# Scattering the weighted FFN rows with addition onto the result in DRAM, instead of reading them back and combining them

## What is computed

```python
gout = x @ Wgate + bgate
topv, topi = jax.lax.top_k(gout, K)              # K = 2 of E = 8 experts
topw = jax.nn.softmax(topv, axis=-1)
combine = jnp.sum(jax.nn.one_hot(topi, E) * topw[..., None], axis=-2)
z = (x @ W1[e] + b1[e]) * (x @ W2[e] + b2[e])    # for each expert e
g = z @ Wg[e] + bg[e]
o = g * sigmoid(g) * (z @ Wl[e] + bl[e])
y = o @ W3[e] + b3[e]
out = einsum('bse,bseh->bsh', combine, y)        # weighted sum of a row's two experts
x = x + attention(xn) + out
```

## Time and profile before

| | |
|---|---|
| median of three runs | 509.82 us |
| the profiled execution's own time | 512.48 us |
| its span in the trace | 510.1 us |
| busy: PE, DVE, ACT, POOL | 401.6, 286.8, 157.0, 228.0 us |
| first gather of the layer-1 FFN starts | 315.4 us |
| its last scatter starts | 487.59 us |
| last entry in the chain that ended last | 503.29 us |

### The profile page before, as it was taken

One profiled execution on the slowest core, in us unless ns is written; L12 is line 12 of the kernel. 1 busy time (PEld: TensorE's weight loads), 2 busy tenths in 40 slices (PEclk: granted clock), 3 DMA queues, 4 the chain that ended last, 5 costly groups with the idle time before them and its releaser, 6 DMA issues.

```text
span 510.1 us, 8068 instructions
## 1 busy us (share of the span) xinstructions
PE 401.6 (79%) x2156; PEld 290.2 (57%) x2157; DVE 286.8 (56%) x791; ACT 157.0 (31%) x414; POOL 228.0 (45%) x341
## 2 busy tenths in 40 slices
PE   2877788999989999476429958799999999998800
PEld 0666677978887877365417626545555555554400
DVE  5246967767657762000084798556666665555514
ACT  1522333434433334133106231232323222222212
POOL 8336516165256234536313012225565666666222
PEclk9988899999999999879759997999999999999955
DMA  8750000000000001967242000001111100001053
GB/s 290 248 229 0 2 1 2 1 0 1 2 2 0 1 21 61 383 243 259 68 152 84 1 0 12 21 12 33 36 31 34 33 31 31 31 31 36 21 155 107
DMA packets 23130, 34.49 MB, mean 68 GB/s; under 512 B 2784, under 2 KB 18400, under 8 KB 22848
## 3 DMA queue, kind: packets, MB, share of 16 engines
q1 hardware_dynamic: 19264, 25.89, 14.7%
q0 software_dynamic: 3840, 8.26, 5.2%
HBM read 26.35 MB, written 7.80 MB: 67 GB/s over the span
## 4 chain that ended last, share of the span: by engine, by line
PE 26%; POOL 24%; issue 23%; DVE 12%; DMA 8%; ACT 2%; POOLq 1%; SPq 1%; another core or an unknown queue 1%; DVEq 0%; ACTq 0%
POOL xg L527 6%; POOL y_rows L542 5%; POOL shared L472 5%; POOL shared L468 4%; PE bank L1202 4%; DMA b2e<-in_b 3%; PE bank L812 3%; PE bank L952 2%; PE bank L914 2%; DMA xg<-xn_rows,ig 2%; POOL isc L539 2%; PE bank L1196 1%; POOL ig L524 1%; DMA xnT<-y_rows 1%; PE bank L936 1%
## 5 line engine op out<-in xcount | busy, mean ns | idle before, releaser
L1202 PE MATMUL bank<-w1s,kexp 128*128 x156 | 76.0, 610 | 1.7 <-ACT kexp L783 1.7
L1391 DVE TENSOR_REDUCE rmax<-bank 128x8 f32<-128x512 f32 (+2 forms) x48 | 30.2, 629 | 50.5 <-PE bank L914 27.6
L542 POOL DMA_INDIRECT y_rows<-ysb,isc x40 | 40.6, 1015 | 32.7 <-POOL isc L539 23.7
L527 POOL DMA_INDIRECT xg<-xn_rows,ig x40 | 39.7, 992 | 31.6 <-POOL ig L524 13.5
L1202 PEld LDWEIGHTS bank<-w1s,kexp 128*128 128x128 f32 x156 | 27.3, 189 | 46.0 <-issue 45.9
L812 PE MATMUL bank<-cb 128*128 128x512 bf16 x97 | 28.8, 428 | 26.5 <-DVEq L1246 15.7
L792 ACT ACTIVATE at<-qf 128x256 f32<-128x256 f32 x39 | 16.2, 416 | 107.9 <-DVE qf L1637 72.4
L1624 DVE TENSOR_TENSOR aT<-bank,shared 128x512 f32<-128x512 f32 x39 | 27.0, 692 | 37.6 <-PE bank L1196 35.7
L952 PEld LDWEIGHTS bank<-shared,w1s 128*128 128x128 f32 x256 | 33.7, 196 | 12.9 <-issue 11.3
L1196 PE MATMUL bank<-w1s,xtT 128*128 x78 | 40.8, 605 | 0.0
L477 POOL TENSOR_TENSOR w1s<-gkgv,cf 64x128 f32<-64x128 f32 x8 | 3.7, 466 | 81.8 <-ACT gkgv L652 81.8
(11 more groups left out here) (238 smaller groups left out, 871.3 us busy)
## 6 DMA issues: line engine op xcount, KB each, us to landing
w1s<-in_w1s SPq DMA_DIRECT2D x2, 3584.0 KB
shared<-in_bias SPq DMA_DIRECT2D x8, 576.0 KB
we<-in_we SPq DMA_DIRECT2D x8, 514.0 KB
xn_rows<-xn SPq DMA_DIRECT2D x8, 256.0 KB, 2.6
xn<-y_rows SPq DMA_DIRECT2D x8, 256.0 KB, 3.9
x<-in_x SPq DMA_DIRECT2D x4, 256.0 KB, 3.5
y_rows<-qe POOLq DMA_DIRECT2D x4, 256.0 KB, 5.2
xnT<-y_rows SPq DMA_DIRECT2D x4, 256.0 KB, 5.6
```

Of the source, the lines that this page charges most:

```text
L527: pool.indirect_dma_start(out=xg[:, slot_b, :], out_offset=None, in_=src, in_offset=bass.IndirectOffsetOnAxis(ap=index.bitcast(U32), axis= ...
L542: pool.indirect_dma_start(out=dst, in_=ysb[:, slot_b, :], in_offset=None, out_offset=bass.IndirectOffsetOnAxis(ap=index.bitcast(U32), axis ...
L1202: mm = pe.matmul(bank[1][:], zT[:, P * a:P * a + P], weights(e, W12 + 2 * F1 * a, 2 * F1), start=(a == 0), stop=(a == 1))
L1391: dve.tensor_reduce(rmax[:, g % 2, :], s3, X, ALU.max).then_inc(s_max, 1)
```

## The change

Each row of `xn1_rows` gets eight more numbers, its share for each expert (0 where it has not chosen that expert). DVE makes them from the one-hot choices and the weights, and SP writes them to DRAM. A gather then brings a row and its shares together. DVE picks the column of the tile's expert (`wcol`), and after y plus bias it multiplies the slot's row by it. The scatter now goes to `out_rows`, a DRAM tensor of N rows plus 128 rows for empty slots, and adds in DRAM. SP has put x of layer 1 (with the attention added) there before. Since a row can be hit by two tiles, and all empty slots of a partition share one row, each scatter waits until the scatter before it has landed. At the end SP copies `out_rows` to `out` from DRAM to DRAM, and the read-back, the products, the sums and the stores from SBUF are gone. `invert` is rearranged, so that a slot's destination is its source row.

```diff
-    f["trash1"] = 2 * N + P * np.arange(J1)[None] + p[:, None]
+    f["trash1"] = np.broadcast_to(N + p[:, None], (P, J1))
...
-    y1_rows = dram("y1_rows", 2 * N + J1 * P)
+    out_rows = dram("out_rows", N + P)
...
@@ SP
-                sp.dma_start(xd[:, 4 * i:4 * i + 4, :], xn[:, 4 * i:4 * i + 4, :]).then_inc(s_xnd, 16)
+                sp.dma_start(xd[:, 4 * i:4 * i + 4, 0:P], xn[:, 4 * i:4 * i + 4, :]).then_inc(s_xnd, 16)
+            sp.wait_ge(s_share, 1)
+            sp.dma_start(xd[:, :, P:], share[:]).then_inc(s_sharein, 16)
+            od = out_rows[0:N, :].rearrange("(t p) d -> p t d", p=P)
+            for i in range(4):
+                sp.wait_ge(s_x2, i + 1)
+                sp.dma_start(od[:, 4 * i:4 * i + 4, :], x[:, 4 * i:4 * i + 4, :]).then_inc(s_rows0, 16)
             for k in range(4):
                 sp.wait_ge(s_ys[k], 16 * (J0 // 4 + (J1 - k + 3) // 4))
-            yd = y1_rows[0:2 * N, :].rearrange("(k t p) d -> k p t d", k=2, p=P)
+            ov, rv = out.rearrange("(p r) d -> p (r d)", p=P), out_rows[0:N, :].rearrange("(p r) d -> p (r d)", p=P)
             for i in range(4):
...
+                sp.dma_start(ov[32 * i:32 * i + 32, :], rv[32 * i:32 * i + 32, :]).then_inc(s_out, 16)
@@ POOL
+            pool.dma_start(out_rows[N:, :], zeros[:, 0:P]).then_inc(s_y0z, 16)
...
             def tile(q, k, single):
                 i = 4 * q + k
                 if not single or k + 3 < J1:
                     pool.wait_ge(t_x, i)
-                    gather(xn1_rows, from1, i + 3, (J0 + i + 3, k + 3))
+                    pool.wait_ge(t_wc, i)
+                    gather(xn1_rows, from1, i + 3, (J0 + i + 3, k + 3), P + E)
+                if single and k == 3:
+                    pool.wait_ge(s_rows0, 64)
                 if not single or 4 <= k:
                     pool.wait_ge(t_ysb, i - 3)
-                    scatter(y1_rows, to1, i - 4, (J0 + i - 4, k - 4))
+                    pool.wait_ge(s_ys[(k - 5) % 4], 16 * (q + (J0 // 4 + (k - 5) // 4 + 1)))
+                    scatter(out_rows, to1, i - 4, (J0 + i - 4, k - 4), compute_op=ALU.add)
@@ DVE, routing
+            own.mark(dve.tensor_tensor(share[:], oh[:], over_e(w1c[:]), ALU.mult))
+            tt(ta[:], oh2[:], over_e(w2c[:]), ALU.mult)
+            tt(share[:], share[:], ta[:], ALU.add)
+            dve.sem_inc(s_share, 1)
@@ DVE, invert
-                stt(rb[:, 0:width], ra[:, 0:width], float(P), trash, ALU.subtract, ALU.subtract)
-                tt(rb[:, 0:width], rb[:, 0:width], rocc[:, 0:width], ALU.mult)
-                own.mark(dve.tensor_tensor(to, rb[:, 0:width], trash, ALU.add))
                 ts(ra[:, 0:width], ra[:, 0:width], float(P), ALU.subtract, 0.0, ALU.max)
                 ts(rb[:, 0:width], ra[:, 0:width], float(N), ALU.is_ge, float(-N), ALU.mult)
-                tt(frm, ra[:, 0:width], rb[:, 0:width], ALU.add)
+                tt(ra[:, 0:width], ra[:, 0:width], rb[:, 0:width], ALU.add)
+                own.mark(dve.tensor_copy(frm, ra[:, 0:width]))
+                tt(rb[:, 0:width], ra[:, 0:width], trash, ALU.subtract)
+                tt(rb[:, 0:width], rb[:, 0:width], rocc[:, 0:width], ALU.mult)
+                tt(to, rb[:, 0:width], trash, ALU.add)
@@ DVE, tile
                     dve.wait_ge(t_h, i + 1)
+                    if not single or k >= 4:
+                        dve.wait_ge(t_ysb, i - 3)
+                    dve.tensor_copy(wcol[:, k % 4:k % 4 + 1], xg[:, k % 4, bass.ds(P + expert_of(q, k), 1)]).then_inc(t_wc, 1)
...
-                    dve.tensor_tensor(ysb[:, (k - 3) % 4, :], bank[5][:, 0:P], bias_y, ALU.add).then_inc(t_ysb, 1)
+                    dve.tensor_tensor(ysb[:, (k - 3) % 4, :], bank[5][:, 0:P], bias_y, ALU.add).then_inc(t_yb, 1)
+                    dve.wait_ge(t_yb, i - 2)
+                    dve.tensor_scalar(ysb[:, (k - 3) % 4, :], ysb[:, (k - 3) % 4, :], wcol[:, (k - 3) % 4:(k - 3) % 4 + 1], None, ALU.mult).then_inc(t_ysb, 1)
```

More of the change, by code:

```diff
@@ L186, in sem, with dram @@
         return ctx.enter_context(nc.semaphore(name))
-    def dram(name, rows):
-        return nc.dram_tensor(name, [rows, P], F32, kind="Internal").ap()
-    xn0_rows, xn1_rows = dram("xn0_rows", N), dram("xn1_rows", N)
+    def dram(name, rows, width=P):
+        return nc.dram_tensor(name, [rows, width], F32, kind="Internal").ap()
+    xn0_rows, xn1_rows = dram("xn0_rows", N), dram("xn1_rows", N, P + E)
     y0_rows = dram("y0_rows", N + J0 * P)
-    y1_rows = dram("y1_rows", 2 * N + J1 * P)
+    out_rows = dram("out_rows", N + P)
     with ctx:
@@ L262, in program @@
         b2e = sb("b2e", [P, 2, P])
-        xg, xgT = sb("xg", [P, 4, P]), sb("xgT", [P, 2 * P])
+        xg, xgT = sb("xg", [P, 4, P + E]), sb("xgT", [P, 2 * P])
+        share, wcol = sb("share", [P, T, E]), sb("wcol", [P, 4])
         hT = sb("hT", [P, 4, 2 * P])
@@ L326, in program @@
         s_parts = sem("bk_parts_ready")
-        s_stats, s_quarter, s_last_quarter = (sem(n) for n in ("statistics_ready", "quarter_added", "last_quarter_added"))
+        s_stats, s_quarter = sem("statistics_ready"), sem("quarter_added")
         s_hit, s_ids = sem("slot_tile_hit"), sem("high_parts_ready")
@@ L334, in program @@
             sem("t_" + n) for n in ("x", "xTs", "h", "hb", "z", "zT", "zTs", "g", "gb", "sil", "o", "oT", "oTs", "y", "ysb"))
-        s_yk = [sem(f"y1_back{i}") for i in range(4)]
-        s_second, s_res, s_out = sem("second_shares"), sem("result"), sem("out_done")
+        s_share, s_sharein, s_rows0, t_wc, t_yb, s_out = (sem(n) for n in (
+            "shares_ready", "shares_in_dram", "x2_in_dram", "t_wcol", "t_yb", "out_done"))
         block = ctx.enter_context(nc.Block())
@@ L514, in _, with gather @@
             pool.wait_ge(s_parts, 8)
-            def gather(src, frm, j, k):
+            def gather(src, frm, j, k, width=P):
                 slot_b = k[1] % 4
@@ L527, in gather, with scatter @@
                 pool.indirect_dma_start(
-                    out=xg[:, slot_b, :], out_offset=None, in_=src,
+                    out=xg[:, slot_b, 0:width], out_offset=None, in_=src,
                     in_offset=bass.IndirectOffsetOnAxis(ap=index.bitcast(U32), axis=0)
                 ).then_inc(s_xg[slot_b], 16)
-            def scatter(dst, to, j, k):
+            def scatter(dst, to, j, k, **how):
                 slot_b = k[1] % 4
@@ L543, in scatter @@
                     out=dst, in_=ysb[:, slot_b, :], in_offset=None,
-                    out_offset=bass.IndirectOffsetOnAxis(ap=index.bitcast(U32), axis=0)
+                    out_offset=bass.IndirectOffsetOnAxis(ap=index.bitcast(U32), axis=0), **how
                 ).then_inc(s_ys[slot_b], 16)
@@ L585, in _ @@
             pool.wait_ge(s_xnd, 128)
+            pool.wait_ge(s_sharein, 16)
             for j in range(3):
-                gather(xn1_rows, from1, j, (J0 + j, j))
+                gather(xn1_rows, from1, j, (J0 + j, j), P + E)
             def tile(q, k, single):
@@ L794, in _ @@
             tile_turns(act, tile)
[L796 to L800, removed]
         @block.tensor
@@ L1047, in turn_rows @@
                     pe.wait_ge(s_xg[kb % 4], 16 * (k[0] + kb // 4 + 1))
-                    mm = pe.transpose(bank[0][:, P * s:P * s + P], xg[:, kb % 4, :], ident)
+                    mm = pe.transpose(bank[0][:, P * s:P * s + P], xg[:, kb % 4, 0:P], ident)
                 mm.then_inc(s_tx, 1)
@@ L1158, in _ @@
                     pe.wait_ge(s_xg[0], 16 * (J0 // 4 + 1))
-                    pe.transpose(bank[6][:, 0:P], xg[:, 0, :], ident).then_inc(t_x, 1)
+                    pe.transpose(bank[6][:, 0:P], xg[:, 0, 0:P], ident).then_inc(t_x, 1)
                 if i >= 3:
@@ L1193, in tile @@
                     pe.wait_ge(s_xg[(k + 1) % 4], 16 * (q + J0 // 4 + (k + 1) // 4 + 1))
-                    pe.transpose(bank[6][:, 0:P], xg[:, (k + 1) % 4, :], ident).then_inc(t_x, 1)
+                    pe.transpose(bank[6][:, 0:P], xg[:, (k + 1) % 4, 0:P], ident).then_inc(t_x, 1)
                 if not single or k < J1:
```

32 lines of the change are left out of this document (1 added, 31 removed).

## The result

The changed kernel takes **527.22 us** (median of four runs, 525.99 to 530.26), the kernel before 509.60 beside it (508.58 to 510.95): a ratio of 1.035, 95% interval 1.030 to 1.040. The forecast was 521, range 503 to 548. The sign and the range hold, and 6 us of the size are missing. (L is the time from the start of an adding scatter to its landing, as in the prediction; the drain is the stretch of the last seven scatters, and DRAIN in capitals is the instruction with which an engine ends its program.)

The account below looks back on a forecast made before the run. No single engine was taken to bound the whole kernel; POOL's cycle paced the loop's end. Terms +1.5 ahead, +9.0 loop, +11.2 drain, -10.5 tail gave +11.2 on 509.8, so 521 us, range 503 to 548.

Parts of the forecast that it names:

- A tile takes L + 1.18 us: Tile loop: waiting for the previous scatter's landing makes 31 steps 4.38 us instead of 4.09, +9.0 us.
- POOL's own work doubles: Rival, loop and drain: an adding scatter's descriptors take POOL 2.0 us instead of 1.0; 543 us, chance 0.05.
- the landing time decides: Loop and drain: up to L = 2.91 us the wait is free in the loop, above it 31 us per microsecond.
- L = 3.2: Adding scatter, start to landing: 3.2 us, taken as the middle of two bounds.
- the bounds of 2.55 and 3.8: Landing time L: 2.55 us if reading old rows costs a gather and the sum is free, 3.8 if read precedes write.
- the drain with it: Last seven scatters and landing: each waits for the one before, 31.1 us instead of 19.9, +11.2 us.
- the add is nearly free: Rival, loop and drain: L below 2.74 us hides in POOL's cycle; 506.8 us at L = 2.55, chance 0.25.
- Reading and writing one after the other: Rival, scatter landing: L = 3.8 us gives 544 us; chance 0.10 for L over 3.85.
- The tail: Last landing to span end: a 6.1 us DRAM copy plus a fixed 3.7 us, 9.8 instead of 20.3, -10.5 us.
- Ahead of the loop: Before the first scatter: DVE share instructions +1.0, `invert` +0.2, pipeline fill +0.3, together +1.5 us.
- What I cost at nothing: Wider gathers, share and x writes, DVE's copy and product (about 0.45 us a turn), PE's clock: hidden, no cost.

## Why the prediction was right in sign and short in size

- **"A tile takes L + 1.18 us" (loop, +9.0): wrong in mechanism, and the main miss.** The price of the loop was put on the wait, with POOL's row kept at 1.0. It is POOL's own row, 1.6, with all that stands behind it 0.6 later: a cycle of 4.61, and 31 steps of 4.69 make +18.6, twice the term. The addition alone gives it (4.718), and the wait on top adds 0.002. What held is the smaller form of the rival "POOL's own work doubles": +0.6 where that had +1.0. It had a chance of 0.05, "against it: no row". That no row spoke for it was no reason either: the trace before has no row for an adding DMA at all, and the price on POOL needed bounds just as L did.
- **Why L didn't show in the loop.** At L = 3.24 the landing needs 4.42 a step (4.48 at the 3.3 of the trace's rows), less than POOL's new 4.61. So the forecast of L was right and did not decide; the title "the landing time decides" holds for the drain only.
- **L = 3.2 (measured 3.24): right**, between the bounds of 2.55 and 3.8, and the drain with it (+12.5 for +11.2, of which 0.9 is the one step of 4.91). It was the middle of two bounds, neither of which had a row of its own, so that it came out to 0.04 is partly luck. The HBM Reference of the Trainium skill (§ Latency) gives 0.2 us for an average access, and the estimate from that figure was L = 2.44; the measurement is 1.0 over the plain scatter, so the page's figure doesn't price a read, an addition and a write.
- **The rival "the add is nearly free": fallen** (L = 3.24 is over 2.9). But the run with tiles written out shows its condition from the other side: without the wait and the index copies an addition is free.
- **"Reading and writing one after the other": fallen**, with L under 3.8.
- **The tail (-10.5, measured -13.9): a term mis-sized.** The copy was right (5.95 for 6.1). The end was not fixed: 3.5 us of it were POOL's closing DRAIN, which is now hidden.
- **Ahead of the loop (+1.5, measured -2.6): not the edit.** The first scatter is at 339.4 to 345.2 in the fourteen profiles. Its mean is 342.4 in the four kernels that have the change ahead of the loop, and 342.4 in the ten that haven't. So the -2.6 lies within the spread of the profiles. The term of +1.5 doesn't show, but one of its size can't be excluded from so few.
- **"What I cost at nothing": held, for the loop as it is.** 544-byte rows, x to `out_rows` (landing 2.3), the DVE instructions and PE's clock (1.00) cost nothing at 4.69 a step. DVE's cover was POOL's slow cycle: once that is gone the changed kernel's other edits, by the rows above DVE's added instructions and their waits, are worth 0.35 us a step (4.094 against 3.749). The forecast said "25.55 busy in 40 us" and counted 0.45 more; the chain also has 0.7 us from the product to the next copy, which no busy share shows.

The errors partly cancel: -4.1 ahead, +9.6 in the loop, +1.3 in the drain, -3.4 in the tail, 3.4 in all, and 3 us more in how the profiled executions stand to the medians. That the loop's miss of 9.6 shows as only 6 in the total is luck, not a property of the forecast.

**What stays open.** What of POOL's 1.6 us is making descriptors and what is waiting for room was not measured. Every kernel with adding scatters has one step, the 25th of the loop, about 1 us longer than the others (5.63 in the changed kernel, 5.65 at half the bytes, 5.17 and 5.19 written out), and no run looked for its cause. The trace shows where the microsecond lies: between the finished index copy and the scatter, 1.84 us and not 0.81, where the program has no wait but the one for that copy (the releaser named in the row had long been done):

```profile
456.22 0.20 POOL L538 COPY isc<-to 128x1 int32 x1
458.26 1.60 POOL L541 DMA_INDIRECT out_rows<-ysb,isc  x1 [1.84 <-PE bank L1182]
```

The cause of the one drain step of 4.91 is open too. A scatter of fewer rows wasn't tried, nor was the changed kernel with its DVE chain shortened.

## What to carry to other kernels

When a change swaps an instruction for a form that the trace has never shown, price its row on the issuing engine as well as its landing, with bounds on each, and ask which of the two the loop feels; they are in different terms of the sum. Before crediting a saved tail, look at which engine ends the program: a DRAIN of 7 to 10 us from POOL's last work on can be the end, and moving the last job off POOL can beat sharing it. And "hidden" is a statement about one pace: what a slow engine covers comes back when it is mended.

## What the runs showed of the hardware that was not expected

- An adding indirect scatter of 128 rows holds POOL for 1.60 us, a plain one 1.00, at 512 and at 256 bytes a row. The small copy behind it has a row that starts within the scatter's, so it reads 0.76 and not 0.20, and ends 0.20 us behind the scatter's. The adding scatter lands 3.24 us after its start, against 2.24, and is, by the difference of the packet counts, 128 packets against 16.
- POOL's closing DRAIN takes 10.2 to 10.4 us in the kernels with plain scatters of layer 1, and 7.0 to 8.0 in those with adding ones, though these have more packets. Its row begins about where POOL's last row does (0.2 us before a last scatter, with a last sum).
- With POOL's 43 turns written out the loop goes from 4.09 to PE's 3.75 us a step, and the kernel is 1.1% shorter. What goes are two one-column copies a tile and the 0.8 us from each to its DMA; 0.3 us from a scatter to the next gather stay.
